# A cross-attention and routed-experts kernel on Trainium2: how rows enter a batch of attention, where gates are ordered, and in what order results are gathered

## The chip, the cores and the metric

The kernel runs on 1 core of one Trainium2 chip. The metric is the device time of that core in microseconds (us), lower is better. Below, PE is TensorE (PEld its weight loads), DVE is VectorE, ACT is ScalarE, POOL is GpSimd, SP is SyncE; a row that ends its engine's name in q is one of the engine's sequencer, mostly a DMA that it issues.

## The reference, cut to what matters

Eight batches of 512 latents (256 wide) attend to 1024 context rows each with 16 heads of 64; the result goes through a router that picks 8 of 64 experts for each of the 4096 tokens.

```python
def attention(latents, context):              # b=8, n=512, s=1024, 16 heads of 64
    lat, ctx = layer_norm(latents), layer_norm(context)
    q, k, v = lat @ Wq, split(ctx @ Wkv)
    k = apply_rope(k, cos, sin)
    attn = softmax(clip(q k^T / 8, -11, 11))
    return (attn v) @ Wo + bo

x = x + tanh(g_xattn) * attention(layernorm(x), ctx)
xf = layernorm(x)
scores = sigmoid(xf @ router_w.T)             # 4 of 8 groups, then 8 of 64 experts
routed = sum over the 8 chosen e of weight_e * (relu(xf @ up[e])**2 @ down[e])
shared = relu(xf @ shared_up)**2 @ shared_down
x = x + tanh(g_ffn) * (routed + shared)
```

## The kernel before

Four stages follow each other, each a block of its own with a barrier behind it.

**setup** splits the projection weights into a high and a low part, turns the rope tables, and normalises the rows of batch 0.

**attention** (line 690) goes over 8 batches of 8 pairs of heads. A pair has eight steps c = 0 to 7. In step c of pair g the PE makes the scores of pair g-1 (L908), the projections of pair g (L939 keys, L951 queries, L924 values), the product with the values (L965), and in steps 1, 4 and 6 the denominator (L973) and the output projection (L1001) of pair g-2. ACT takes the exponential (L1043) and copies projections out of PSUM, POOL clips the exponentials (L1147) and finishes keys (L1143), DVE sums exponentials (L1336), does rope (L1320, L1321), the low halves (L1326, L1308) and 1/denominator (L1311, L1313). The value projection runs in the first two of every four pairs; the last two have less work for the PE. Since a loop always has a pair before it, the first pair attends to a zeroed pair: keys, queries, values and two exponentials are filled with zeros at the start. The routing of batch b-1 (the functions of `Router`) is spread over the pairs of batch b on DVE, and its rows are scattered to DRAM by POOL.

Between two batches stands `boundary(b)`: the PE turns the normalised rows of the new batch in three units of eight 128x128 transposes into the two score buffers (L887), ACT and DVE each apply the layer norm's gain and shift to half a unit (L1020, L1278), ACT writes the high part (L1024), DVE the low part (L1285). The new batch's first scores wait for it, since the buffers are those of the scores. Batch 0 is a hardware loop of its own, that normalises one tile at a time; the later batches normalise two.

**finish_routing** does the shared expert for all tokens and routes the last batch. DVE there also orders the gates: for each of 32 tiles of tokens three operations of 128x512 (compare the slots with the keys, multiply with the gates, reduce to 8 gates). Tiles 0 to 15 are wholly DVE's (L1568, L1570, L1571); for tiles 16 to 31 (`by_pool`) the multiplication is POOL's (L1443), between DVE's L1578 and L1588, into space that is free only after the last scatter.

**experts** goes over 320 blocks of 128 rows. For each block the PE turns the rows (L1814), multiplies with the up weights (L1787) and the down weights (L1807); DVE does relu and square (L1845, L1849) and every second copy to the result ring (L1839), ACT the other copies. SP loads rows, stores results in groups of four blocks (L1716), and loads the down weights of four experts with every second one of the first 32 blocks. POOL gathers the results of a batch of tokens, 32 gathers for each of 8 batches (L1870), each of one choice k of one tile of tokens into one of 8 buffers, in the order k = 0 to 7, and DVE adds them (L1832), one gather's rows beside each block. A batch's gathers begin when all blocks that its rows may lie in have been stored:

```python
            def gather(b):
                for k in range(YR // YC):
                    pool.wait_ge(y_stored[k], (b * BODY + E_R + BODY) // YR * 16)
                for q in range(BODY):
                    t, k = q // TOP_K, q % TOP_K
```

with BODY = 32, E_R = 64, YR = 8 and YC = 4. The keys of a token are its slots sorted downwards, so k = 7 is the smallest slot, and slots of one expert's later tokens lie higher in memory.

## Time and profile before

| | us |
|---|---|
| median of 3 runs | 2625.3 (2624.1 to 2625.47) |
| the profiled execution's own time | 2619.68 |
| its span, first to last instruction | 2617.9 |
| setup, to the start of attention's block | about 33 |
| attention | to about 1992 |
| finish_routing | to about 2163 |
| experts | to 2617.9 |

The granted TensorE clock over the span is 0.957 of full speed, where 1.00 is 2.4 GHz and 0.5 is 1.2 GHz. The chain of waits and the groups of instructions give averages over stages that have different limits, so each stage is read by itself, by the timeline and by the busy time of its stretches.

### The profile page before, as it was taken

Reading aid. Unit: us, or ns where it says so; the run is one execution under the profiler, and the core shown is the slowest. Engines: PE = TensorE matmul, PEld = TensorE weight load, DVE = VectorE, ACT = ScalarE, POOL = GpSimd, SP = SyncE. Lnnn points to the kernel's source line nnn. Section 1 sums busy time; section 2 is a strip of 40 time slices with the busy share of each in tenths; the row PEclk is TensorE's granted clock in tenths of the full one; section 3 lists DMA queues with packets and bytes.
Section 4 is the critical chain, followed back from the end, with each engine's and each line's share of the span. In section 5 each row is a group of like instructions: output and inputs, shape, how many; then the busy total and the mean of one; then the engine's idle time right before and its main releaser. Section 6 shows DMA issues by size and latency. Waiting matters only on the chain. (4 is left out here: it accounts for less than half of the span.)

```text
span 2617.9 us, 41338 instructions
## 1 busy us (share of the span) xinstructions
PE 2320.2 (89%) x11459; PEld 1289.8 (49%) x11459; DVE 2104.3 (80%) x3593; ACT 1518.0 (58%) x2536; POOL 1800.0 (69%) x1569
## 2 busy tenths in 40 slices
PE   2999899999989999998999899999997958999990
PEld 1444444444544444444444444444444647988770
DVE  5687688988897897889889878988896775688884
ACT  3666666666665666666666656666662423666660
POOL 3787576679858885887698688858875630077776
PEclk9999999999999999999999999999997989999995
DMA  8434333221111111111211111111115408799994
GB/s 301 170 105 167 114 125 101 77 79 43 59 46 59 55 59 46 59 44 53 79 43 57 48 57 56 60 46 57 45 55 172 150 1 305 243 321 325 328 319 141
DMA packets 163129, 305.71 MB, mean 117 GB/s; under 512 B 19842, under 2 KB 99138, under 8 KB 160194
## 3 DMA queue, kind: packets, MB, share of 16 engines
q1 hardware_dynamic: 134786, 235.40, 26.5%
q0 software_dynamic: 24576, 67.14, 7.7%
q8 instruction: 107, 1.75, 0.3%
q14 instruction: 140, 1.15, 0.1%
q10 hardware_dynamic: 3520, 0.27, 0.1%
HBM read 172.99 MB, written 129.76 MB: 116 GB/s over the span
## 5 line engine op out<-in xcount | busy, mean ns | idle before, releaser
L1147 POOL TENSOR_SCALAR e<-e 128x1024 f32<-128x1024 f32 x520 | 682.2, 1312 | 364.5 <-ACT e L1043 311.2
L1043 ACT ACTIVATE e<-scores 128x1024 f32<-128x1024 f32 x520 | 533.2, 1025 | 443.8 <-PE scores L908 437.1
L1336 DVE TENSOR_TENSOR e_sum<-e_sum,e 128x1024 f32<-128x1024 f32 x391 | 612.7, 1567 | 107.7 <-POOL e L1147 103.1
L965 PE MATMUL ps_o<-e,v 128*64 128x512 f32 x2088 | 570.3, 625 | 6.8 <-POOL e L1147 6.8
L908 PE MATMUL scores<-q_t,k_t 64*128 64x512 f32 x3120 | 512.6, 434 | 14.4 <-ACT affine L1020 12.7
L908 PEld LDWEIGHTS scores<-q_t,k_t 64*128 64x128 f32 x3120 | 257.9, 188 | 378.5 <-issue 313.4
L1870 POOL DMA_INDIRECT more<-results_in_blocks,index x256 | 246.4, 962 | 210.6 <-DMA results_in_blocks<-more 129.4
L1055 ACT ACTIVATE k_sw<-ps_k 32x512 f32<-32x512 f32 x512 | 301.2, 588 | 83.5 <-PE ps_k L939 78.7
L1132 POOL DMA_INDIRECT rows_in_blocks<-room,a_r_index_now x192 | 265.5, 1383 | 49.0 <-issue 42.1
L939 PE MATMUL ps_k<-ctx_t,wqk 128*128 128x512 f32 x768 | 222.9, 427 | 12.5 <-DVE q_t L1308 12.2
L924 PE MATMUL ps_v<-wv,ctx_t 128*128 128x512 f32 x768 | 212.1, 411 | 0.0
L1143 POOL TENSOR_TENSOR k_c<-k_c,k_sw 128x512 f32<-128x512 f32 x128 | 194.8, 1521 | 19.9 <-DVE k_sw L1321 17.2
L965 PEld LDWEIGHTS ps_o<-e,v 128*64 128x64 f32 x2088 | 104.5, 136 | 201.4 <-issue 172.0
L1001 PE MATMUL ps_y<-wo,o_n 128*128 128x256 f32 x528 | 158.4, 425 | 48.0 <-POOL o_n L1151 46.7
L1807 PE MATMUL ps_out<-down_all,room 128*128 (+1 forms) x640 | 194.1, 385 | 3.3 <-DVE room L1849 2.4
L939 PEld LDWEIGHTS ps_k<-ctx_t,wqk 128*128 128x128 f32 x768 | 141.0, 197 | 87.2 <-issue 44.7
L1001 PEld LDWEIGHTS ps_y<-wo,o_n 128*128 128x128 f32 x528 | 94.1, 198 | 168.1 <-POOL o_n L1151 89.8
L1814 PE MATMUL ps_x<-ident,x_nat 128*128 128x128 f32 x640 | 125.4, 278 | 50.2 <-PEq L1351 27.6
L1326 DVE TENSOR_TENSOR k_t<-k_c,k_t 128x512 fp32r<-128x512 f32 x128 | 125.6, 981 | 53.7 <-ACT k_t L1068 53.5
L924 PEld LDWEIGHTS ps_v<-wv,ctx_t 128*128 128x128 f32 x768 | 134.2, 188 | 69.8 <-issue 47.0
L1770 ACT ACTIVATE x_nat<-ps_x 128x256 f32<-128x256 f32 x320 | 121.2, 379 | 76.9 <-PE ps_x L1814 73.4
L1832 DVE SCALAR_TENSOR_TENSOR x<-more,gate,x 128x256 f32<-128x256 f32 x256 | 123.1, 481 | 48.0 <-DMA more<-results_in_blocks,index 46.6
(294 smaller groups left out, 3612.3 us busy)
## 6 DMA issues: line engine op xcount, KB each, us to landing
rows_in_blocks<-room SPq DMA_DIRECT2D x16, 2560.0 KB, 10.1
x_nat<-rows_in_blocks SPq DMA_DIRECT2D x160, 256.0 KB, 5.2
results_in_blocks<-more SPq DMA_DIRECT2D x80, 512.0 KB
wqk<-wqk_pairs SPq DMA_DIRECT2D x65, 512.0 KB, 3.5
wv<-wv_quads SPq DMA_DIRECT2D x17, 1024.0 KB, 4.9
wo<-in_L_xattn_Wo SPq DMA_DIRECT2D x66, 128.0 KB, 3.4
x_nat<-in_ctx SPq DMA_DIRECT2D x8, 1024.0 KB, 7.7
down_all<-in_L_ffn_down_w SPq DMA_DIRECT2D x16, 512.0 KB, 8.2
```

What stands on the lines that cost most here:

```text
L908: mm = pe.matmul(scores[:, c % 2, hh * N:(hh + 1) * N], k_t[rows, att, kp, c * P:(c + 1) * P], q_t[rows, att, qp, :], start=(part == 0), s ...
L924: mm = pe.matmul(ps_v[:], ctx_t[:, a, cc, tile * P:(tile + 1) * P], wv[:, bb, cc], start=(k == 0), stop=(k == 5))
L939: mm = pe.matmul(ps_k[:], wqk[:, jj, bb, cc, 1], ctx_t[:, a, cc, half * N:(half + 1) * N], start=(k == 0), stop=(k == 5))
L965: mm = pe.matmul(ps_o[hh * DH:(hh + 1) * DH, :], v[:, tile, buf, hh * DH:(hh + 1) * DH], e[:, tile % 4, hh * N:(hh + 1) * N], start=(tile ...
L1001: mm = pe.matmul(ps_y[:, i, :], o_n[:, t * P:(t + 1) * P], wo[:, jj], start=True, stop=True)
L1043: act.activation(e[:, c % 4], scores[:, c % 2], ACT.Exp, scale=SCALE).then_inc(s_exp, 1)
L1055: st = act.activation(k_sw[to], ps_k[of], ACT.Copy)
L1132: pool.indirect_dma_start(xs_dram, bass.IndirectOffsetOnAxis(ap=router.index_now[:, t, k:k + 1], axis=0), router.rows[:, t], None).then_in ...
L1143: pool.tensor_tensor(k_c[:], k_c[:], k_sw[:], ALU.add).then_inc(s_turned, 1)
L1147: pool.tensor_scalar(e[:, c % 4], e[:, c % 4], EXP_HI, EXP_LO, ALU.min, ALU.max).then_inc(s_clip, 1)
L1336: dve.tensor_tensor(total, e[:, 0] if c == 2 else total, e[:, tile % 4], ALU.add).then_inc(s_sum, 1)
L1870: pool.indirect_dma_start(land[:, k], None, y_dram[0:(E_R + (b + 1) * BODY) * P, :], bass.IndirectOffsetOnAxis(ap=at, axis=0)).then_inc(y_ ...
```

## The change

**Six pieces instead of a boundary.** `boundary` is gone from all engines. The rows of the next batch are turned in six pieces of four transposes, each of 128x512 elements, into the buffer of the value projection (`ps_v`), five in steps 3 to 7 of the last pair of the batch and the sixth in step 0 of the first pair of the next. For each piece ACT applies gain and shift and writes the high part, DVE writes the low part. DVE no longer has a share of the gains.

**No empty pairs.** The first pair has no scores, exponentials, sums and outputs; the pair's code is left out where there is no pair g-1 or g-2, and the fills with zeros are gone. Semaphores are raised to the counts that would have been. Batch 0 is written out as the others are. The first five pieces of batch 0 stand ahead of the loop, and DVE waits for all rows of x behind them. SP's first loads no longer wait for the fills. The router's weights and biases are loaded and turned in `setup`.

**Order inside a pair.** At step 2 ACT takes the logarithm of the denominator ahead of the exponential, DVE's two operations for 1/denominator come right behind the sum of step 2 (before: step 3, behind the low half of the query), and at step 3 POOL multiplies with it ahead of its clip.

**Gates.** Tiles 16 to 31 are ordered in finish_routing, all by DVE, where tiles 0 to 15 were; tiles 0 to 15 are ordered in the first 48 blocks of experts, one of the three operations in each block. POOL has no part in it any more. Slots and gates are kept in halves, so four loads and two scalings stand where two loads and one scaling were.

**Gathers.** A tile's choices are gathered from k = 7 down, and the gathers for k = 7 to 4 of a batch's first tile need one group of four blocks less.

**First down weights.** The down weights of experts 0 to 3 are also loaded at the end of finish_routing, behind the scatters, into space of their own, and the first four blocks use these.

```diff
-                for k in range(YR // YC):
-                    pool.wait_ge(y_stored[k], (b * BODY + E_R + BODY) // YR * 16)
                 for q in range(BODY):
-                    t, k = q // TOP_K, q % TOP_K
+                    t, k = choice(q)
+                    n = blocks_of(b, k) // YC
+                    if q in (0, YC):
+                        for group in (n - 2, n - 1):
+                            pool.wait_ge(y_stored[group % (YR // YC)], (group // (YR // YC) + 1) * 16)
...
+        def choice(q):
+            return q // TOP_K, TOP_K - 1 - q % TOP_K
+        def blocks_of(b, k):
+            return -(-(E_R + (b + 1) * BODY - k) // YC) * YC
...
+        CHUNKS = 6
+        CHUNK_AT = {(7, 3): 0, (7, 4): 1, (7, 5): 2, (7, 6): 3, (7, 7): 4, (0, 0): 5}
...
+            def turn_rows(n, number):
+                pe.wait_ge(s_affine, 1 + number)
+                for t in range(NT):
+                    mm = pe.transpose(ps_v[:, t * P:(t + 1) * P],
+                                      x_nat[:, (0, 4, 8)[n // C2] + t, n % C2 * P:(n % C2 + 1) * P], pers.ident[:])
+                mm.then_inc(turned, 1)
...
+            def place_rows(n, number):
+                k = chunk_of(n, 0)[1]
+                act.wait_ge(turned, number + 1)
+                if not isinstance(number, int) or number >= 2:
+                    act.wait_ge(t_lo, number - 1)
+                act.activation(affine[:, n % 2], ps_v[:], ACT.Identity, bias=pers.shift[:, k, n % C2:n % C2 + 1],
+                               scale=pers.gain[:, k, n % C2:n % C2 + 1]).then_inc(s_affine, 1)
+                act.wait_ge(s_affine, 1 + number + 1)
+                act.activation(chunk_of(n, 0)[0], affine[:, n % 2], ACT.Copy).then_inc(t_hi, 1)
...
+            def split_rows(n, number):
+                dve.wait_ge(t_hi, number + 1)
+                dve.tensor_tensor(chunk_of(n, 1)[0], affine[:, n % 2], f32(chunk_of(n, 0)[0]), ALU.subtract
+                                  ).then_inc(t_lo, 1)
+            for n in range(CHUNKS - 1):
+                split_rows(n, n)
+            dve.wait_ge(x1_loaded, 16 * (B - 1))
...
+            sp.dma_start(router.rows, ins["down_w"][0:CHUNK].rearrange("e p n -> p e n")).then_inc(kept.first_loaded, 16)
...
+                if i < 3 * LATER:
+                    order(i)
```

How the change moves instructions is seen at three places. The first is the PE's program at the passage from the last pair of a batch (steps 6 and 7) to the next batch. Before (L887 are the boundary's transposes, L908 scores, L965 values, L793 the loop's turn):

```order
L908 MATMUL scores<-q_t,k_t 128x512 x6
L965 MATMUL ps_o<-e,v 64x512 x2
L1001 MATMUL ps_y<-wo,o_n 128x256 x2
L908 MATMUL scores<-q_t,k_t 128x512 x6
L965 MATMUL ps_o<-e,v 64x512 x2
L793 UNCONDITIONAL_BRANCH
L793 ISA
L880 ISA
L887 MATMUL scores<-ident,x_nat 128x128 x16
L883 ISA
L887 MATMUL scores<-ident,x_nat 128x128 x8
```

and after (L881 are the transposes of one piece, L903 the scores, L968 values):

```order
L903 MATMUL scores<-q_t,k_t 128x512 x6
L881 MATMUL ps_v<-ident,x_nat 128x128 x4
L968 MATMUL ps_o<-e,v 64x512 x2
L1004 MATMUL ps_y<-wo,o_n 128x256 x2
L903 MATMUL scores<-q_t,k_t 128x512 x6
L881 MATMUL ps_v<-ident,x_nat 128x128 x4
L968 MATMUL ps_o<-e,v 64x512 x2
L813 UNCONDITIONAL_BRANCH
L813 ISA
L896 REGISTER_ALU
L897 ISA
L903 MATMUL scores<-q_t,k_t 128x512 x6
```

The 24 transposes in a row have become groups of four between the scores and the product with the values of a step.

The second place is DVE's program at the end of finish_routing and the beginning of experts. Before (L1568 to L1571 order one tile, L1845 and L1849 are the first blocks' relu and square; ahead of these rows stand the 16 tiles shared with POOL):

```order
L1568 TENSOR_TENSOR cells<-more,key 128x512
L1570 TENSOR_TENSOR cells<-cells,more 128x512
L1571 TENSOR_REDUCE gate<-cells 128x8
L1351 UNCONDITIONAL_BRANCH
L1825 UNCONDITIONAL_BRANCH
L1845 TENSOR_SCALAR room<-ps_hid 128x128
L1849 TENSOR_TENSOR room<-room 128x128
L1845 TENSOR_SCALAR room<-ps_hid 128x128
L1849 TENSOR_TENSOR room<-room 128x128
```

and after (L1522 to L1525 order one tile, L1506 adds the shared expert's result, L1798 and L1801 are the first two parts of ordering a tile in the first blocks):

```order
L1525 TENSOR_REDUCE gate<-cells 128x8
L1506 SCALAR_TENSOR_TENSOR x<-ps_s,gates,x 128x512 x2
L1310 UNCONDITIONAL_BRANCH
L1776 UNCONDITIONAL_BRANCH
L1810 TENSOR_SCALAR room<-ps_hid 128x128
L1814 TENSOR_TENSOR room<-room 128x128
L1798 TENSOR_TENSOR e_cells<-more,key 128x512
L1810 TENSOR_SCALAR room<-ps_hid 128x128
L1814 TENSOR_TENSOR room<-room 128x128
L1801 TENSOR_TENSOR e_cells<-e_cells,more 128x512
```

No ordering is left behind the last addition of the stage, and one part of it stands in each of the first 48 blocks.

## Rows read from the trace of the kernel before

**Rows 1.** The page: the span and TensorE's busy time (share) and instructions.

```profile
span 2617.9 us, 41338 instructions
PE 2320.2 (89%) x11459; PEld 1289.8 (49%) x11459; DVE 2104.3 (80%) x3593; ACT 1518.0 (58%) x2536; POOL 1800.0 (69%) x1569
```

**Rows 2.** ACT's exponentials by stretch: stretch, length, busy (count), granted clock, DMA share, GB/s.

```profile
1446.80:1482.10 35.30, 8.20 (x8) 0.92 0.10 32
1928.00:1953.70 25.70, 8.21 (x8) 1.00 0.15 47
```

**Rows 3.** Stretches: length; PE, PEld, DVE, ACT, POOL busy (count); clock, DMA share, GB/s.

```profile
1242.20:1273.10 30.90, 30.48 (x135) 15.20 (x136) 25.41 (x37) 19.39 (x28) 16.25 (x12) 0.97 0.18 56
...
1927.80:1953.80 26.00, 23.48 (x112) 10.16 (x110) 25.66 (x30) 16.16 (x22) 20.15 (x15) 1.00 0.15 46
```

**Rows 4.** PE's timeline at a boundary: start, us, line, operation [idle before <-releaser].

```profile
1477.11 1.94 PE L887 MATMUL scores<-ident,x_nat 128*128 128x128 f32 x8 [3.17 <-DVE affine L1278]
1480.47 1.65 PE L908 MATMUL scores<-q_t,k_t 64*128 64x512 f32 x6 [1.42 <-ACT affine L1020]
```

**Rows 5.** Single lines: count, ns min/median/max, first and last start, shapes.

```profile
L1020 ACT ACTIVATE affine<-scores,shift,gain x24: 758/762/779, 51.5 to 1720.6; 128x512 f32<-128x512 f32 x24
L1024 ACT ACTIVATE ctx_t<-affine x32: 612/630/634, 52.4 to 1720.1; 128x512 fp32r<-128x512 f32 x32
L1285 DVE TENSOR_TENSOR ctx_t<-affine,ctx_t x32: 676/682/687, 54.8 to 1721.5; 128x512 fp32r<-128x512 f32 x32
L1326 DVE TENSOR_TENSOR k_t<-k_c,k_t x128: 674/938/1573, 73.8 to 1953.8; 128x512 fp32r<-128x512 f32 x128
```

**Rows 6.** PE's waits over the span: who for whom, us in total, times, longest.

```profile
PE ps_y L1001 <- POOL o_n L1151: 46.7, 37, 4.6
...
PE ps_k L939 <- DVE q_t L1308: 12.2, 6, 2.0
```

**Rows 7.** The timeline at the start of attention.

```profile
39.70 0.34 SPq L808 DMA_DIRECT2D wqk<-wqk_pairs  x1
...
60.08 2.39 ACT L1055 ACTIVATE k_sw<-ps_k 32x512 f32<-32x512 f32 x4 [0.46 <-PE ps_k L939]
60.19 1.74 DVE L1336 TENSOR_TENSOR e_sum<-e_sum,e 128x1024 f32<-128x1024 f32 x1 [0.75 <-DMA x<-in_x]
...
64.63 1.66 PE L951 MATMUL ps_k<-lat_t,wqk 128*128 128x512 f32 x6
...
87.91 1.03 ACT L1043 ACTIVATE e<-scores 128x1024 f32<-128x1024 f32 x1 [0.88 <-PE scores L908]
```

**Rows 8.** The timeline at the end of finish_routing.

```profile
2128.47 7.17 PE L1480 MATMUL ps_s<-sdn,h_g 128*128 128x256 f32 x32 [1.35 <-ACT h_g L1512]
...
2135.68 0.75 DVE L1552 SCALAR_TENSOR_TENSOR x<-ps_s,gates,x 128x512 f32<-128x512 f32 x1 [2.63 <-PE ps_s L1480]
...
2163.22 1.88 PE L1814 MATMUL ps_x<-ident,x_nat 128*128 128x128 f32 x6 [27.58 <-PEq L1351]
```

**Rows 9.** The comparison of one tile's slots, and its timeline neighbours in a block of experts.

```profile
L1568 DVE TENSOR_TENSOR cells<-more,key x16: 677/691/694, 2060.7 to 2160.5; 128x512 f32<-128x512 f32 x16
...
2205.27 0.29 DVE L1845 TENSOR_SCALAR room<-ps_hid 128x128 f32<-128x128 f32 x1 [0.48 <-PE ps_hid L1787]
2205.59 0.29 DVE L1849 TENSOR_TENSOR room<-room 128x128 f32<-128x128 f32 x1
2205.80 0.42 DVE L1839 COPY more<-ps_out 128x256 f32<-128x256 f32 x1
```

**Rows 10.** The blocks' copies L1770 by stretch: columns as in rows 2.

```profile
2163.90:2205.90 42.00, 12.21 (x32) 0.94 1.05 366
...
2205.90:2223.40 17.50, 6.10 (x16) 1.00 0.74 244
```

**Rows 11.** The gathers: line as in rows 5, then the first in the timeline.

```profile
L1870 POOL DMA_INDIRECT more<-results_in_blocks,index x256: 940/946/1212, 2284.8 to 2611.4; - x128
...
2284.80 1.12 POOL L1870 DMA_INDIRECT more<-results_in_blocks,index  x1 [129.44 <-DMA results_in_blocks<-more]
```

498 lines of the change are left out of this document (215 added, 283 removed).

## The prediction, made before the changed kernel ran

> **What bounds the kernel now.** I read the page first: TensorE is busy 89% of a span of 2617.9 us [rows 1]. That is an average over stages, so next come the stages one by one, in stretches and in the timeline. In attention the PE is busy 30.48 of 30.9 us in the first pair of a batch [rows 3], so a pair with value projections is the PE's. The last pair of a batch has none, and there DVE is busy 25.66 of 26.0 us and the PE 23.48 [rows 3]: that pair is DVE's. Behind it stands the boundary. The last pair with a boundary behind it takes 35.3 us, the very last pair, which has none, 25.7 us [rows 2]. In those 9.6 us the PE waits 3.17 us for DVE's share of the gains and 1.42 us for ACT's, and then makes its scores in 1.65 us [rows 4]; the granted clock over the pair and its boundary is 0.92, against 1.00 in the pair without one [rows 2]. At the start of attention the PE has nothing before the fills and router loads are done: the second pair's first exponential starts at 87.91 us [rows 7]. At the end of finish_routing the PE is done, DVE adds the last product at 2135.68 us, and the next stage's first matmul starts at 2163.22 us after 27.58 us of idle PE [rows 8]; between them DVE only orders gates. In experts the gathers are one chain on POOL: 256 of them from 2284.80 to 2611.4 us, (2611.4 - 2284.8) / 255 = 1.28 us each [rows 11], with the rest of the blocks beside them. So what comes before the first gather moves the end, and what comes after it hardly does.
>
> **Start of attention.** The first load is issued at 39.70 us, and DVE waits at 60.19 us for the last rows of x [rows 7]: 20.5 us. Changed, SP issues the first load right behind the barrier, at about 33.2 us, and is 1.7 us shorter, since the three router loads are in setup, where they lie beside larger loads. The rows land at 33.2 + 20.5 - 1.7 = 52.0 us. The first five pieces are done by then (each of them some 1.7 us, from about 34.5 us), so DVE's wait for x is what ends last. Then the first pair, which has no attention to hide behind, runs as a chain. DVE splits the sixth piece and multiplies with the cosine, 0.68 us each as the same shape takes in [rows 5]: 53.4. Query projection 1.66 [rows 7]: 55.0. ACT's copy 0.63, DVE's low half 0.68 [rows 5]: 56.3. Second half of the keys 1.66: 58.0. ACT swaps the key halves in 2.39 us [rows 7] while the first of three value tiles waits to be copied out of the one buffer: 60.4 + 0.6; the two further tiles take 1.66 + 0.63 + about 0.1 of signalling each: 65.6. Scores, about 1 us: the second pair's first exponential starts at 66.6 us instead of 87.9. That is **-21.3 us**. If x did not bind, the same chain would begin 8 us earlier (-29); if it landed as late as now, it would be -13.
>
> **Boundaries.** Seven of them go. What goes with each is 9.6 us [rows 2], and about 0.5 us of slow matmuls in the first step behind it (scores at 1.65 us [rows 4]). What comes for it are six pieces. On the PE each is four transposes; eight take 1.94 us at the slow clock [rows 4], so half a microsecond at the full one, five times 2.5 us, and the PE has 2.5 us of room in the last pair [rows 3]. ACT gets 0.76 + 0.63 = 1.39 us a piece [rows 5], five times 7 us, on 16.16 of 26.0 us [rows 3]: it fits. DVE has no room: 25.66 of 26.0. It gets five low halves. The same subtraction takes 0.682 us at the boundary, where POOL stands still, and 0.938 us as the median among pairs, up to 1.573 [rows 5]. I take 0.94, since the pieces now stand among POOL's clips: 5 x 0.94 = 4.7 us in the last pair. The sixth falls into a pair that the PE bounds [rows 3] and costs nothing as long as that is so. So each boundary becomes 4.7 us, net 10.1 - 4.7 = 5.4, seven times **-37.8 us**. The last batch had no boundary, but turns rows that nobody uses: **+4.7 us**.
> The Trainium skill, page "SBUF — State Buffer", section "Who interferes with whom", speaks against the change here: a DVE instruction with two SBUF inputs contends with a GpSimd instruction that reads SBUF, by an exclusive lock. The two rows for one shape, 0.682 and 0.938 us, agree with it. With 0.68 for each of the five halves the last pair would be 1.3 us shorter, over eight batches 10 us; by the rule the longer value holds.
>
> **Order inside a pair.** POOL's product ahead of its clip takes away some of the PE's waits for it, 46.7 us over the span in 37 places; 1/denominator ahead of the query's low half lengthens the waits for that one, 12.2 us in 6 places [rows 6], where DVE is late, by the two operations of 0.68 us each. It also lets a clip wait where the product is late. I take 0, with 15 us either way at most.
>
> **End of finish_routing.** The 16 tiles with POOL and three tiles behind them leave; the three that stay between the last two groups take 3 x 3 x 0.69 = 6.2 us [rows 9], which is less than the 7.17 us of the products alone that the PE works on meanwhile [rows 8]. The stage ends with DVE's addition at 2135.68 + 0.75 = 2136.4 instead of 2162.7: -26.3 us. The PE's wait of 1.35 us before the last products [rows 8] falls to the usual half microsecond, as DVE is not late any more: -0.8. The extra loads and the extra scaling, five short operations of about 1 us in all, lie beside the PE's matmuls; the scatters end some 50 us before the stage does. Together **-27.1 us**. The early load of four experts' down weights costs nothing there and takes a possible wait from block 0; the other loads are as they were.
>
> **First blocks of experts.** Each of 48 blocks gets one operation of 0.69 us [rows 9] on DVE. A block has relu to square 0.32 us and square to the next start 0.21 us [rows 9], and each second one the copy of 0.42. With 0.61 to 0.69 for the new part a block takes DVE 0.32 + 0.21 + 0.65 + 0.2 = 1.35 to 1.4 us. The first 32 blocks take 42.0 us now, 1.31 each, at a DMA share of 1.05: there the loads bound them [rows 10], and 32 x 1.34 is about 43. The next 16 take 17.5 us, 1.10 each [rows 10]; they become 21.2. Together **+4.7 us**, and everything up to the first gather moves with it. At the bounds: 0, if DVE's part hides behind the loads and in the PE's lag, and 48 x 0.69 = 33 us if nothing hides.
>
> **Gathers.** The first gather may start one group of four blocks earlier, 4 x 1.10 = **-4.4 us** [rows 10]; the fifth waits for the next group, which is 4.4 us later, and four gathers take 5.1 us. The chain behind it has as many gathers as before. Bounds: 0 and -5.
>
> **Sum.** -21.3 - 37.8 + 4.7 + 0 - 27.1 + 4.7 - 4.4 = -81.2 us. The profiled execution took 2619.7 us, 1.8 more than its span and 5.6 less than the median of the runs; on that median, 2625.3 - 81.2 = 2544.1 us.
>
> **Rivals.** All keep the start, the stage end and the gathers (-21.3 - 27.1 + 4.7 - 4.4 = -48.1) and differ in what six pieces cost, x, against 10.1 us a boundary: -48.1 + 7 (x - 10.1) + x.
> *Pieces hidden.* DVE's lag in the last pair is carried into the next pair, where DVE is busy only 25.41 of 30.9 us [rows 3]; then x is 2 or less. For it: nothing but the next denominator waits for DVE's sums. Against it: that denominator comes in step 1. With x = 2: 2625.3 - 102.8 = 2522.5 us.
> *Pieces as dear as the boundary.* DVE late by 1/denominator as well, the PE waiting for the query's low half, ACT held up behind a turn that waits for the piece before. x = 10.1: 2625.3 - 38.0 = 2587.3 us. For it: that pair already holds the PE's waits for the low half of the query.
> *Slower.* One buffer, one affine tile of two halves and in-order queues make each piece a serial chain on the path: transposes 0.5, gains 0.76, high part 0.63, low part 0.94, 2.83 us; six make x = 17.0. Then 2625.3 - 48.1 + 48.3 + 17.0 = 2642.5 us. It decides against the change from x = 15.6, where -48.1 + 7 x 5.5 + 15.6 is +6. Against it: the scores have buffers of their own, so PE, ACT and DVE can work on different pieces.
> *Ordering exposed.* As forecast, but the first blocks lose 15 to 33 us instead of 4.7, if the added part delays each relu, and with it the PE's next block: 2554 to 2572 us. Against it: two blocks are in flight between PE and DVE.
>
> **How the numbers follow.** Forecast 0.57 (its own range 2530 to 2558), hidden pieces 0.19, dear pieces 0.09, exposed ordering 0.12, slower 0.03. The range 2515 to 2575 takes in the hidden pieces, the start at either bound (+8, -8) and most of the exposed ordering; it leaves out the dear pieces and the slower case, about 0.15 with what lies below. About 0.2% (5 us) is what a measurement of this kernel can tell from no change. Faster by more than that 0.96, within it 0.01, slower 0.03.
>
> **What would show it.** Right: the second pair's first exponential near 66.6 us; eight exponentials of a batch's last pair in 30 to 31 us with DVE full; PE idle for about 1 us instead of 27.58 at the start of experts; 32 blocks in about 43 us and 16 in 21; gathers again at 1.28 us each. Wrong: PE waits on ACT or DVE lines of the pieces, a last pair above 33 us, a wait of DVE for x that ends past 55 us, or blocks above 1.5 us each while the gates are ordered.

## The result and the profile after

The changed kernel takes 2555.4 us (median of 4 runs, 2553.0 to 2559.0); the kernel before took 2624.7 us beside it (4 runs, 2622.7 to 2625.5). The ratio is 0.9738, with a 95% interval of 0.9721 to 0.9755, and 69 us are gone where 81 were forecast. The profiled execution has a span of 2551.4 us for 2617.9 [rows 1]. One execution behind the medians below is left out: the fourth of number_late took 2639.5 us at a granted clock of 0.835, where its other three had 0.97.

The page, its span and first lines (columns as in rows 1):

```profile
span 2551.4 us, 40379 instructions
PE 2294.6 (90%) x11366; PEld 1273.0 (50%) x11366; DVE 2055.1 (81%) x3571; ACT 1524.2 (60%) x2556; POOL 1734.6 (68%) x1515
```

TensorE has 25.6 us less to do and still shows 90%: the average says next to nothing here, as before. So the two traces are laid side by side by stage. Each number of this table is the difference, after minus before, between two events of the profiled executions:

| stretch | forecast us | measured us |
|---|---|---|
| up to the second pair's first exponential (87.91, 67.02) | -21.3 | -20.9 |
| from there to the last pair of batch 0 (162.7, 156.0 long) | 0 | -6.7 |
| from there to the attention tail's first exponential (1953.8, 1906.0) | -33.1 | -20.2 |
| from there to the first block of experts (2163.9, 2091.8) | -27.1 | -24.3 |
| from there to the first gather (120.9, 120.7 long) | +4.7 - 4.4 | -0.2 |
| first to last gather (326.6, 332.3 long) | 0 | +5.7 |
| sum | -81.2 | -66.6 |

The third row and the last one are off by 12.9 and 5.7 us, and the second one, which was to be 0, takes 6.7 us back. For the third row, the exponentials of a last pair and of the pair 0 behind it (columns as in rows 2):

```profile
923.70:956.90 33.20, 8.18 (x8) 0.95 0.10 34
956.90:988.30 31.40, 8.26 (x8) 1.00 0.17 56
1875.10:1906.00 30.90, 8.19 (x9) 0.94 0.12 40
```

The very last pair, which had taken 25.7 us [rows 2], takes 30.9; the one with a pair 0 behind it 33.2, where the forecast was 30.4. It is the dearest of its kind; the seven take 31.3 us in the mean. The same stretches with all engines (columns as in rows 3):

```profile
923.70:956.90 33.20, 29.73 (x142) 14.16 (x144) 31.41 (x35) 22.49 (x32) 19.30 (x16) 0.95 0.10 34
1875.10:1906.00 30.90, 28.12 (x134) 12.87 (x134) 29.21 (x32) 22.41 (x33) 19.28 (x16) 0.94 0.12 40
```

DVE is busy 31.41 of 33.2 us, so the pair is still DVE's; but the PE has become dearer too, 28.1 us for 23.48 [rows 3], at a granted clock of 0.94 for 1.00. Four transposes at 0.66 us, five times, are 3.3 of these 4.6 us (the forecast had 0.5 us for each four). Another 0.9 stands behind one wait, where four matmuls of the product with the values take 1.98 us for 1.08. PE's waits over the span, as in rows 6:

```profile
PE ps_k L944 <- DVE q_t L1264: 34.1, 20, 2.7
...
PE ps_y L1004 <- POOL o_n L1135: 17.8, 9, 3.6
```

The wait for POOL's product went from 46.7 to 17.8 us, the wait for the query's low half from 12.2 to 34.1. That fits the new order inside the pair, which the forecast had put at 0; the experiments test it. One such wait, first on the PE, then in DVE's queue (timeline, columns as in rows 4):

```profile
939.47 2.50 PE L944 MATMUL ps_k<-ctx_t,wqk 128*128 128x512 f32 x6 [2.71 <-DVE q_t L1264]
```

```profile
929.30 1.05 DVE L461 TENSOR_TENSOR a_r_at_next<-room,a_r_ranks 128x64 f32<-128x64 f32 x1
930.38 0.23 DVE L463 TENSOR_TENSOR a_r_over<-a_r_at_next,room 128x64 f32<-128x64 f32 x1
930.64 0.19 DVE L468 TENSOR_SCALAR a_r_opened<-a_r_over 128x64 f32<-128x64 f32 x1
930.87 3.44 DVE L471 SCALAR_TENSOR_TENSOR a_r_opened<-a_r_over,a_r_opened 128x64 f32<-128x64 f32 x3
934.26 1.23 DVE L1286 TENSOR_TENSOR e_sum<-e 128x1024 f32<-128x1024 f32 x1
935.40 0.68 DVE L1289 TENSOR_TENSOR o_n<-ps_y,r_den 128x512 f32<-128x512 f32 x1
936.12 0.69 DVE L1291 SCALAR_TENSOR_TENSOR r_den<-o_n,r_den 128x512 f32<-128x512 f32 x1
936.73 2.09 DVE L478 TENSOR_TENSOR a_r_opened<-a_r_opened 128x64 f32<-128x64 f32 x3
938.74 0.68 DVE L1264 TENSOR_TENSOR q_t<-ps_k,q_t 128x512 fp32r<-128x512 f32 x1
```

DVE has no gap in these rows. In the last pair the router's block counts (L461 to L478) stand in step 1 and 2, and the low half of the query, whose high half ACT had finished at 932.4 us, comes at 938.74 behind all of it. The PE stands still for 2.71 us, and the projection behind the wait takes 2.50 us, at a granted clock of 0.62, where it takes 1.65 at the full clock.

### The profile page after: what moved, and what is told of

It is laid out like the page before. It is cut to its first block and busy times, and to the rows that moved or that the text cites. A ratio compares the mean times of both kernels' runs of the same rounds, so it can differ in the third digit from the quotient of the medians.

```text
span 2551.4 us, 40379 instructions
## 1 busy us (share of the span) xinstructions
PE 2294.6 (90%) x11366; PEld 1273.0 (50%) x11366; DVE 2055.1 (81%) x3571; ACT 1524.2 (60%) x2556; POOL 1734.6 (68%) x1515
## 3 DMA queue, kind: packets, MB, share of 16 engines
q1 hardware_dynamic: 135234, 235.93, 27.1%
## 5 line engine op out<-in xcount | busy, mean ns | idle before, releaser
L1139 POOL TENSOR_SCALAR e<-e 128x1024 f32<-128x1024 f32 x512 | 689.8, 1347 | 357.5 <-ACT e L1047 303.6
L1047 ACT ACTIVATE e<-scores 128x1024 f32<-128x1024 f32 x512 | 525.1, 1026 | 410.9 <-PE scores L903 398.2
L1286 DVE TENSOR_TENSOR e_sum<-e_sum,e 128x1024 f32<-128x1024 f32 x384 | 585.7, 1525 | 160.7 <-POOL e L1139 151.9
L968 PE MATMUL ps_o<-e,v 128*64 128x512 f32 x2048 | 560.8, 626 | 7.0 <-POOL e L1139 6.6
L903 PE MATMUL scores<-q_t,k_t 64*128 64x512 f32 x3072 | 499.9, 431 | 4.7 <-issue 4.7
L903 PEld LDWEIGHTS scores<-q_t,k_t 64*128 64x128 f32 x3072 | 251.4, 186 | 365.2 <-issue 293.2
L944 PE MATMUL ps_k<-ctx_t,wqk 128*128 128x512 f32 x768 | 219.4, 422 | 34.1 <-DVE q_t L1264 34.1
L968 PEld LDWEIGHTS ps_o<-e,v 128*64 128x64 f32 x2048 | 102.7, 136 | 192.1 <-issue 161.1
L1004 PE MATMUL ps_y<-wo,o_n 128*128 128x256 f32 x512 | 154.6, 427 | 21.1 <-POOL o_n L1135 17.8
L1004 PEld LDWEIGHTS ps_y<-wo,o_n 128*128 128x128 f32 x512 | 92.1, 200 | 138.4 <-issue 94.8
L1734 PE MATMUL ps_hid<-x_nat,room 128*128 128x128 f32 x1024 | 156.5, 275 | 2.0 <-DVE room L1810 1.2
```

The lines of the kernel that those rows point to most:

```text
L903: mm = pe.matmul(scores[:, c % 2, hh * N:(hh + 1) * N], k_t[rows, att, kp, c * P:(c + 1) * P], q_t[rows, att, qp, :], start=(part == 0), s ...
L944: mm = pe.matmul(ps_k[:], wqk[:, jj, bb, cc, 1], ctx_t[:, a, cc, half * N:(half + 1) * N], start=(k == 0), stop=(k == 5))
L968: mm = pe.matmul(ps_o[hh * DH:(hh + 1) * DH, :], v[:, tile, buf, hh * DH:(hh + 1) * DH], e[:, tile % 4, hh * N:(hh + 1) * N], start=(tile ...
L1004: mm = pe.matmul(ps_y[:, i, :], o_n[:, t * P:(t + 1) * P], wo[:, jj], start=True, stop=True)
L1047: act.activation(e[:, c % 4], scores[:, c % 2], ACT.Exp, scale=SCALE).then_inc(s_exp, 1)
L1139: pool.tensor_scalar(e[:, c % 4], e[:, c % 4], EXP_HI, EXP_LO, ALU.min, ALU.max).then_inc(s_clip, 1)
```

## The experiments

All times are medians; the kernel before, run beside them, had medians of 2622.4 to 2623.5 us. Where an effect has a place of its own, it is read there. For the batches this table gives, per kernel, the seven last pairs that have a batch behind them, the seven pairs 0 behind those, and the very last pair, all from first exponential to first exponential in the profiled execution, and their sum:

| kernel | median us | ratio, 95% interval | seven last pairs | seven pairs 0 | very last pair | sum |
|---|---|---|---|---|---|---|
| before | 2624.7 | | 248.1 | 216.2 | 25.8 | 490.1 |
| changed | 2555.4 | 0.9738 (0.9721 to 0.9755) | 219.0 | 224.2 | 30.9 | 474.1 |
| no_pieces | 2529.9 | 0.9646 (0.9627 to 0.9665) | 204.3 | 213.4 | 29.6 | 447.2 |
| no_low | 2546.8 | 0.9711 (0.9691 to 0.9730) | 218.5 | 219.1 | 30.6 | 468.2 |
| pieces_early | 2554.8 | 0.9736 (0.9719 to 0.9752) | 224.1 | 221.4 | 31.8 | 477.3 |
| den_back | 2521.8 | 0.9620 (0.9604 to 0.9636) | 202.0 | 215.6 | 27.8 | 445.3 |
| order_back | 2539.8 | 0.9678 (0.9662 to 0.9694) | 206.5 | 218.1 | 28.6 | 453.1 |
| before_order | 2642.9 | 1.0072 (1.0052 to 1.0092) | 265.3 | 219.9 | 28.7 | 513.8 |
| number_late | 2536.5 | 0.9676 (0.9657 to 0.9696) | 205.4 | 221.7 | 28.3 | 455.4 |
| low_on_pool | 2540.1 | 0.9689 (0.9673 to 0.9705) | 215.9 | 218.4 | 29.4 | 463.8 |
| start_and_last | 2509.8 | 0.9569 (0.9553 to 0.9585) | 200.4 | 217.4 | 24.0 | 441.8 |
| finish_late | 2505.7 | 0.9551 (0.9538 to 0.9564) | 196.7 | 214.4 | 23.0 | 434.1 |
| gates_back | 2583.7 | 0.9851 (0.9831 to 0.9871) | 217.2 | 225.3 | 30.6 | 473.0 |
| gather_old | 2553.6 | 0.9735 (0.9719 to 0.9752) | 218.9 | 224.9 | 30.6 | 474.4 |

The last two have the attention of the changed kernel, unchanged, so their sums show what one profiled execution differs from another by: 473.0 to 474.4. Not every profile lies near its median: den_back's took 2515.3 us, 6.5 less than the median of its four.

**Are the pieces too dear, or is it the order?** First the pieces were taken away as a whole, then DVE's part of them.

```diff
-                    turn_rows(n, number)
+                    if left_out(b, p):
+                        pe.wait_ge(s_affine, 1 + number)
+                        pe.sem_inc(turned, 1)
+                    else:
+                        turn_rows(n, number)
...
-                    place_rows(*chunk)
+                    # the same on ACT: wait for turned, count s_affine and t_hi
...
-                    split_rows(*chunk)
+                    # the same on DVE: wait for t_hi, count t_lo (in no_low this one alone)
```

> The six pieces of every batch are left out (their transposes, gains, high and low halves; only the counting of their semaphores stays), but for the first six at the start; so every batch attends to the rows of the first, and the routing that comes of it is another one. To be read is the first exponential of the attention tail, 1906.0 us in the changed kernel. The prediction had 33.1 us less for boundaries and pieces, and the traces show 20.3 less. Theory one, the pieces are dearer than the 4.7 us a batch that were forecast: with 7 (x - 10.1) + x = -20.3 they cost x = 6.3 us a batch, and without them the tail's first exponential comes 8 x 6.3 = 50 us earlier, near 1856. Rival, the pieces cost the forecast 4.7 us and the missing 12.8 us are the new order inside the pair (1/denominator ahead of the query's low half): then 8 x 4.7 = 38 us earlier, near 1868.

Measured: the tail's first exponential at 1882.2 us, 23.8 earlier, which is 3.0 us a batch. Both theories fall: with the new order the pieces cost less than even the forecast's 4.7 us a batch, and without any the very last pair still takes 29.6 us, where the kernel before takes 25.8. PE's wait for the query's low half is all there without pieces:

```profile
PE ps_k L952 <- DVE q_t L1277: 37.3, 20, 3.9
```

> Only the low halves of the pieces on DVE are left out in the loop (six a batch; the transposes, the gains and the high halves stay), so the low halves of the rows stay those of the first batch. Read at the tail's first exponential, 1906.0 us. Theory one, the last pair is DVE's and a piece costs what DVE does for it: 5 x 0.94 us in each last pair and what the sixth costs in the next, 40 to 50 us in all, so 1856 to 1866. Rival, a piece is a serial chain through ACT and the one buffer (gains 0.76, high half 0.63), and DVE's part is hidden: less than 15 us, so 1891 or later.

Measured: 1902.4 us, 3.6 earlier. That is the rival's number, though perhaps not for its reason: with the changed order PE waits for the query's low half in any case, and the same edit with the old order, which would tell, was not run.

**Other places for the pieces.**

```diff
-        CHUNK_AT = {(7, 3): 0, (7, 4): 1, (7, 5): 2, (7, 6): 3, (7, 7): 4, (0, 0): 5}
+        CHUNK_AT = {(7, c): c - 1 for c in range(1, CHUNKS + 1)}
...
```

> All six pieces stand in the batch's last pair, in steps 1 to 6 instead of 3 to 7 and the next batch's step 0 (the order of them becomes first half of the context, queries' rows, second half). Theory one: pair 0 after a boundary (31.3 to 33.7 us against 30.9 to 31.3 before) pays for the sixth piece and for what the last pair hands over, and the last pair, DVE's, pays 0.94 us for each piece: pair 0 falls by about 1.5 us, the last pair rises by 0.9; over seven batches -4 us, at the very last batch +0.9: the whole 2 to 5 us faster. Rival: the pieces in steps 1 and 2 stand in front of the query projection, 1/denominator and its two waits, and the last pair lengthens by more than the 1.5 us: 0 to 10 us slower.

Measured: 2554.8 us, no difference. Over seven batches pair 0 gets 2.8 us shorter and the last pair 5.1 us longer, partly made up elsewhere. Of these two placements, with the new order, neither is better.

**The order inside the pair.** On DVE alone it goes back:

```diff
@@ DVE, step 2, behind the sum
-                if c == 2 and tail:
-                    dve.wait_ge(s_seed, g + 1)
-                    dve.tensor_tensor(o_n[:], y_flat, r_den[:], ALU.mult).then_inc(s_part, 1)
-                    ...
@@ DVE, step 3, behind the query's low half
+                if c == 3 and tail:
+                    dve.wait_ge(s_seed, g + 1)
+                    ...
```

> On DVE alone the two operations of 1/denominator go back behind the low half of the query, one step later; on ACT and POOL the order stays the changed one. Theory one, that move costs: the PE's key projection waited 34.1 us in 20 places for that low half (12.2 us in 6 before); with the move undone this falls to about 12, the whole is 10 to 20 us faster. Rival, it moves the wait: POOL's product, now ahead of its clip, gets 1/denominator later and holds up the clip, and the PE's value products with it; PE waits for clips and for POOL's product rise by as much or more: 0 to 20 us slower.

Measured: 2521.8 us, 33.6 faster, more than theory one gave it. The same place of the same batch, DVE and PE:

```profile
920.35 3.43 DVE L471 SCALAR_TENSOR_TENSOR a_r_opened<-a_r_over,a_r_opened 128x64 f32<-128x64 f32 x3
923.72 1.22 DVE L1292 TENSOR_TENSOR e_sum<-e 128x1024 f32<-128x1024 f32 x1
924.87 0.74 DVE L478 TENSOR_TENSOR a_r_opened<-a_r_opened 128x64 f32<-128x64 f32 x3
925.52 0.68 DVE L1264 TENSOR_TENSOR q_t<-ps_k,q_t 128x512 fp32r<-128x512 f32 x1
926.12 0.68 DVE L1267 TENSOR_TENSOR o_n<-ps_y,r_den 128x512 f32<-128x512 f32 x1
```

```profile
926.26 1.67 PE L944 MATMUL ps_k<-ctx_t,wqk 128*128 128x512 f32 x6
```

From the sum to the query's low half DVE now takes 1.80 us instead of 4.48. Two operations of 0.68 us explain 1.4 of the 2.7. The other 1.35 is the numbering of blocks (L478), 0.74 us for 2.09: with 1/denominator late, POOL stands still beside it (it ends a clip at 923.45 us and starts its product at 927.62), and the three operations run undisturbed. The PE does not wait, and its projection takes 1.67 us. POOL's wait for 1/denominator is the longer for it, but PE's waits for POOL's product are 20.9 us in all, 17.8 in the changed kernel. The last pair of batch 0, beside which DVE has nothing to route yet, takes 27.2 us in both kernels; that of the fourth batch, shown above, takes 33.2 and 29.7. So in the last pairs the move costs only in the batches that route, with the router's operations in DVE's queue as well. The cost is not confined to the last pairs: of the 28.8 us between the two sums in the table, 17.0 are in the seven last pairs, 8.6 in the pairs 0 and 3.1 in the very last one. POOL's wait in den_back:

```profile
927.62 1.64 POOL L1135 TENSOR_TENSOR o_n<-o_raw,r_den 128x256 f32<-128x256 f32 x1 [4.17 <-DVE r_den L1269]
```

With the order back on all three engines:

```diff
@@ besides den_back: ACT, step 2
                     act.activation(q_t[:, jj, 0], ps_k[:], ACT.Copy).then_inc(s_qe, 1)
+                # the logarithm and the exponential of 1/denominator, from ahead of it
@@ POOL, step 3
+                # the product o_n behind the clip, from ahead of it
```

> The whole order inside the pair is the old one again: on DVE 1/denominator behind the query's low half, on ACT its logarithm and exponential behind the query's copy, on POOL the product behind the clip. The run with DVE's part alone undone (called den_back) took 2521.8 us, 33.6 less than the changed kernel. Theory one, DVE's part is the whole cost, and what ACT and POOL got is a small gain of its own (the PE's waits for POOL's product were 46.7 us before and 17 with the product ahead of the clip): this run is 5 to 25 us slower than den_back, 2527 to 2547. Rival, the order hurts on each engine, ACT and POOL too: this run is faster than den_back, below 2520 us.

Measured: 2539.8 us, 18.0 slower than den_back. Theory one holds: beside DVE's old order, what ACT and POOL got is a gain of 18.0 us; on top of that, what DVE got is a loss of 33.6, and the whole order costs 15.6 us. (DVE's move alone, without ACT's and POOL's, was not run in the changed kernel, so the two parts are told in this order only.) PE's wait for the product is back:

```profile
PE ps_y L1004 <- POOL o_n L1139: 48.3, 40, 4.6
```

And the new order in the kernel before, without pieces, start or gates:

```diff
@@ the kernel before: ACT, step 2, ahead of the step's exponential; its second half behind it
+                    act.activation(r_den[:], y_flat, ACT.Ln).then_inc(s_log, 1)
@@ DVE, from step 3 to step 2, behind the sum; POOL, step 3, ahead of the clip
+                    dve.tensor_tensor(o_n[:], y_flat, r_den[:], ALU.mult).then_inc(s_part, 1)
+                    pool.tensor_tensor(o_n[:, 0:D], o_raw[:, 0:D], r_den[:, 0:D], ALU.mult).then_inc(s_on, 1)
```

> The kernel before with one edit, the new order inside the pair on ACT, DVE and POOL. Theory one: DVE's move costs in the last pair, where the router's block counts stand in DVE's queue as well, whether there are pieces or not (the changed kernel without pieces takes 10.3 us in step 4 of that pair, with DVE's move undone it is 5.2 us): the kernel before becomes 20 to 35 us slower, about 2650, and its last pairs 3 to 4 us longer. Rival: the cost comes only of pieces and order together, both on DVE in one pair: the kernel before stays within 8 us of 2624.

Measured: 2642.9 us, 18 to 20 slower, just short of theory one's 20 to 35 and far from the rival's 8, and close to the 15.6 that it costs in the changed kernel. Its last pairs are 2.5 us longer each, less than theory one had (3 to 4), pair 0 another 0.5. The waits trade in the same way (12.2 and 46.7 before, [rows 6]):

```profile
PE ps_k L939 <- DVE q_t L1308: 34.2, 19, 3.9
...
PE ps_y L1001 <- POOL o_n L1147: 17.1, 8, 3.6
```

Does it take 1/denominator to make the low half late, or only a long queue?

```diff
-                if (p, c) == (7, 2):
+                if (p, c) == (7, 3):
                     router.number_blocks(dve, range(0, 3))
```

> One edit to the changed kernel: the router's numbering of blocks, three operations on DVE, moves from step 2 to step 3 of the last pair, so that it stands behind the query's low half; 1/denominator stays ahead of it. Theory one: the PE waits for that low half because of all that is queued ahead of it on DVE, whichever it is; 2.1 us less of it (three operations of 0.7 us with POOL busy) take 2 us off the wait in each of seven last pairs and about 0.9 us off the projection behind it, which ran at the low clock (2.50 us for 1.66): 14 to 20 us faster, step 4 of the last pair 8.6 to about 6 us. Rival: it is the chain of 1/denominator itself (the seed from ACT, then two operations, POOL behind them) that sets step 4, and the numbering only fills a wait: less than 4 us.

Measured: 2536.5 us, 18.9 faster, and step 4 of the last pair 5.4 us for 8.5 in the mean of the six batches that route. Theory one holds: moving other work from ahead of the low half helps too, so it does not take 1/denominator.

**The start of experts.**

```diff
+            for k in range(GT):
+                dve.wait_ge(router.scattered[k], 16 * TOP_K * N_G)
+            order(range(0, LATER))
@@ experts
-                if i < 3 * LATER:
-                    order(i)
```

> The sixteen tiles of gates that the changed kernel orders in the first 48 blocks of experts are ordered at the end of finish_routing instead, by DVE alone (the kernel before had POOL's help there and took 27.6 us of idle PE); all else as changed. Theory one, as predicted: 48 operations of 0.69 us stand on the path at the stage's end, 33 us more between DVE's last addition and the first block, and the first 64 blocks get faster again, 81.4 back to 77.2 us: 33 - 4.2 = 29 us slower, near 2584. Rival: the head start of the blocks is given back later, as it was with the gathers, since the gathers' chain waits for stored groups: less than 20 us slower.

Measured: 2583.7 us, 28.3 slower. The first block's wait, 35.95 us for 1.11, and the first 64 blocks, 77.2 us for 81.5, bear out both terms. They make 30.6 us; in the trace 2.8 of them are given back behind the ninth gather (312.1 us to the last one, for 314.9), much less than the rival had:

```profile
2125.82 1.09 PE L1768 MATMUL ps_x<-ident,x_nat 128*128 128x128 f32 x4 [35.95 <-PEq L1310]
```

**The gathers.**

```diff
-            return q // TOP_K, TOP_K - 1 - q % TOP_K
+            return q // TOP_K, q % TOP_K
...
-            return -(-(E_R + (b + 1) * BODY - k) // YC) * YC
+            return E_R + (b + 1) * BODY
```

(and the waits for the stored groups once ahead of each batch, as in the kernel before.)

> In experts the gathers go again from the largest slot down, each batch of them behind all the groups of blocks that it may need; all else as changed. The first gather then starts about 4.4 us later against the first block (120.7 us after it in the changed kernel). Theory one, the head start is given back: in the changed kernel the first 32 gathers took 48.3 us for 44.0 before, waiting for stored groups, since blocks are made no sooner; the end moves by less than 2 us. Rival, as the prediction had it, the head start reaches the end: 4.4 us slower.

Measured: 2553.6 us, the same within the interval. POOL in the changed kernel, its first, its eighth and its ninth gather; then the eighth and ninth with the old order:

```profile
2212.53 1.00 POOL L1839 DMA_INDIRECT more<-results_in_blocks,index  x1 [171.89 <-DMA results_in_blocks<-more]
...
2221.60 0.95 POOL L1839 DMA_INDIRECT more<-results_in_blocks,index  x1 [0.30 <-issue]
2229.93 0.95 POOL L1839 DMA_INDIRECT more<-results_in_blocks,index  x1 [7.38 <-DVE x L1783]
```

```profile
2224.88 0.95 POOL L1837 DMA_INDIRECT more<-results_in_blocks,index  x1 [0.30 <-issue]
2228.95 0.94 POOL L1837 DMA_INDIRECT more<-results_in_blocks,index  x1 [3.13 <-DVE x L1783]
```

The head start is given back, but not where theory one had it. The ninth gather needs the place of the first one in SBUF, so it waits for DVE's first addition, and that stands in DVE's program behind block 112 (64 + 32 + 16), wherever the gathers are. Counted from the first block, the first gather starts after 120.7 us (125.3 with the old order), the ninth after 138.2 (138.4).

**The start of attention and the last batch.**

```diff
@@ DVE
-            dve.wait_ge(x1_loaded, 16 * (B - 1))
...
+                    if isinstance(b, int) and b == 0 and p == 1 and c == 0:
+                        dve.wait_ge(x1_loaded, 16 * (B - 1))
@@ the loop
-            with eng.Fori(2, B) as b:
-                batch(b)
+            with eng.Fori(2, B - 1) as b:
+                batch(b)
+            with eng.Fori(B - 1, B) as b:
+                batch(b)          # without pieces, norms and the load of the next batch
```

> Three edits to the changed kernel. 1/denominator on DVE is back behind the query's low half (2521.8 us as the only edit). DVE's wait for the rows of x of the later batches moves from ahead of the loop to their first reader, the moments in pair 1 of batch 0. The last batch gets a copy of the loop of its own, without the pieces, the load and the normalising of a batch that does not come. Each can be read in its own place. The start: x lands at 51.5 us in the changed kernel while DVE is ready at about 47.2; theory one, the second pair's first exponential comes 4 us earlier, near 63; the rival, x takes the wait along to whichever reader and the PE's slow clock sets the pair: less than 1 us. The last batch's last pair takes 27.8 us in the run with the only edit; theory one, 25.7 to 26, as in the kernel before, and another 0 to 3 us from the normalising in pairs 3 and 5; rival, a third copy of the loop's code has to be fetched and eats the gain. Together 2514 by theory one, 2522 by the rivals.

Measured: 2509.8 us, 12.0 faster than den_back. At the start the rival is right, 66.6 us for 67.4. In the changed kernel x is what DVE waits for; without that wait it waits for ACT's swap, behind a projection at the lower clock, and is 0.4 us earlier:

```profile
51.53 0.69 DVE L1163 TENSOR_TENSOR ctx_t<-affine,ctx_t 128x512 fp32r<-128x512 f32 x1 [4.71 <-DMA x<-in_x]
52.14 0.68 DVE L1270 TENSOR_TENSOR k_c<-ps_k,cos_t 128x512 f32<-128x512 f32 x1
```

```profile
48.37 0.69 DVE L1168 TENSOR_TENSOR ctx_t<-affine,ctx_t 128x512 fp32r<-128x512 f32 x1 [1.29 <-ACT ctx_t L1026]
51.72 0.69 DVE L1282 TENSOR_TENSOR k_c<-ps_k,cos_t 128x512 f32<-128x512 f32 x1 [2.66 <-ACT k_sw L1070]
```

(Nine kernels with one and the same start have 67.0 to 68.0 us there, this one and finish_late 66.6 and 66.5.) The last batch gives the larger part: its last pair takes 24.0 us instead of 27.8, and its eight pairs 223.7 instead of 230.7, 7.0 us less; it leaves out three things at once, and they are not told apart. Where the other 4 us of the 12.0 lie, these profiles do not show.

**Low halves on POOL.**

(Besides DVE's edit of den_back.)

```diff
@@ POOL, last pair, behind the clip (and no longer on DVE)
+                    pool.wait_ge(t_hi, number + 1)
+                    pool.tensor_tensor(chunk_of(n, 1)[0], affine[:, n % 2], f32(chunk_of(n, 0)[0]), ALU.subtract
+                                       ).then_inc(t_lo, 1)
```

> Two edits to the changed kernel: 1/denominator on DVE is back behind the query's low half (2521.8 us as the only edit), and the low halves of the five pieces in the last pair are made by POOL instead of DVE, behind its clip of the step. The last pair is DVE's, and the next pair's first key projection waits 1.7 us for a low half that DVE makes late, with POOL idle for 2.2 us and 3.1 us around it. Theory one: DVE has 5 x 1.2 us less, POOL 5 x 1.5 us more and room for it; each last pair and the pair behind it lose 2 to 3 us together: 15 to 25 us faster than 2521.8. Rival: POOL's subtraction stands ahead of the next clip, and the contended operations on both engines take as much longer as is saved: within 8 us of 2521.8, or slower.

Measured: 2540.1 us, 18.3 slower than den_back. The rival, and worse. Its DVE and POOL in the second half of a last pair:

```profile
947.24 2.31 DVE L1298 TENSOR_TENSOR e_sum<-e_sum,e 128x1024 f32<-128x1024 f32 x1 [1.02 <-POOL e L1139]
```

```profile
943.96 1.18 POOL L1147 TENSOR_TENSOR o_n<-o_raw,r_den 128x256 f32<-128x256 f32 x1
945.22 1.90 POOL L1139 TENSOR_SCALAR e<-e 128x1024 f32<-128x1024 f32 x1
947.20 1.27 POOL L1144 TENSOR_TENSOR ctx_t<-affine,ctx_t 128x512 fp32r<-128x512 f32 x1
948.42 2.25 POOL L1131 TENSOR_TENSOR k_c<-k_c,k_sw 128x512 f32<-128x512 f32 x1
```

POOL has next to no gap in these rows, DVE waits for clips (191.0 us over the span, for 162.9 in den_back), and PE for POOL's products (33.3 us for 20.9). DVE's sum takes 2.31 us where it takes 1.22 alone. In this pair DVE's operations add up to 29.7 us, in den_back's to 31.0: of the 5.7 us that low halves took in it there, some 4.4 came back through operations that both engines run at once.

**DVE's work out of its full stretch.**

(Besides the three edits of start_and_last.)

```diff
-        FINISH = (1, 2, 4, 6, 7)
+        FINISH = (3, 4, 5, 6, 7)
...
                 if part == 0:
                     router.r, router.k = r, numbered[0]
-                    router.number_blocks(dve, range(3, 6))
+                    router.number_blocks(dve, range(0, 6))
...
                 if (p, c) == (7, 2):
-                    router.number_blocks(dve, range(0, 3))
                     numbered[0] = router.k
```

> The three edits of the run start_and_last (2509.8 us) and a fourth: the router's numbering of blocks on DVE, three operations in step 2 of the last pair and three in step 1 of the next pair 0, all moves to step 3 of pair 0, and the two parts of slot work behind it one step later each (steps 4 and 5 for 2 and 4). In start_and_last DVE has no idle time from step 6 of pair 6 to step 3 of pair 0, and the last pair takes 29.7 us where the PE has work for 26. Theory one: what counts is DVE's work in that full stretch, wherever it stands in it; 4.8 us less of it (2.1 in the last pair, 2.7 in pair 0) make the last pair and pair 0 together 2 to 4 us shorter, seven times: 2482 to 2496 us. Rival: the slot work ends later, POOL's wait for the slots at the start of pair 1 holds up its clips, and pair 1 (29.3 us) pays what the others gain: within 4 us of 2509.8.

Measured: 2505.7 us (5 runs, 2503.4 to 2509.3), 4.1 faster than start_and_last and so between the theories, nearly the rival's; the intervals of the two ratios overlap. In the batches the gain is there, 3.7 us over the last pairs and 3.0 over pairs 0, about 1 us each time and not the 2 to 4 of theory one; pair 1 stays at 29.3 to 30.0 us, so the rival's place is wrong. The attention tail, from its first to its last exponential, takes 24.6 us for 22.2; whether the later slot work is the cause is not shown, for the three kernels with one and the same attention have 23.1, 25.8 and 25.9 us there. It has the lowest median of this study, 49.7 us faster than the changed kernel and 4.5% faster than the one before.

## Why the prediction was right, and where its steps were not

The time came out 11 us above the forecast and inside its range, in part by luck. In the trace 14.6 us are missing. Three misses add to it, the third row of the table with 12.9 us, the gathers with 5.7 and finish_routing with 2.8; the 6.7 us that batch 0 lost unforeseen take half of the first away. With the order inside the pair undone, order_back takes 2539.8 us, 4 below the forecast. Of the signs of being wrong that the prediction named, one came: two of the seven last pairs are above 33 us. Step by step:

- **What bounds the kernel** held. The last pair is DVE's, and the reading that a last pair with no boundary would cost 25.7 us plus the pieces is borne out once the order is back: in order_back the last pairs, pairs 0 and the very last pair sum to 453.1 us, 37.0 less than before, where -37.8 + 4.7 = -33.1 were forecast. With 10.1 us a boundary gone, that leaves 4.2 us a batch for the pieces, where the forecast had 4.7: right, a little too careful. It was right by a sum whose parts were not: DVE's five low halves take 5.0 to 6.5 us in a last pair of the changed kernel and 7.2 in most of den_back, not 4.7, so some of it hides.
- **Start of attention** held to 0.4 us (67.02 for 66.6), partly by luck. (The forecast's own chain adds up to 66.8: 60.4 + 0.6 and two times 2.39 are 65.8.) DVE's wait for x ended at 51.53 us for the forecast 52.0. The pieces took 1.98 us each for the assumed 1.7 and the first projections 2.91 us for 1.66, at the lower clock. The forecast's bound, 8 us earlier if x did not bind, was wrong: the PE's and ACT's chain ends within half a microsecond of x, as start_and_last shows.
- **Not forecast**: batch 0 is another 6.7 us shorter up to its last pair. 5.1 of them are in the first of these pairs (24.2 us for 29.4), which has no pair g-2 to finish any more.
- **Order inside a pair** is the step that failed. It took 0 with 15 us either way; undoing it gives 15.6 us, at the edge of that. The two directions were named rightly, but their sizes were not: in den_back and order_back the gain by ACT and POOL is 18.0 us, the loss by DVE 33.6. The forecast sized the loss by the wait as it stood (12.2 us in 6 places), plus two operations of 0.68 us. It left out that these stand in the one pair that its own first part had called DVE's, behind the router's operations; that POOL's product, which then starts earlier, lengthens DVE's operations beside it (the three of the numbering from 0.74 to 2.09 us); and that the PE comes out of some of these waits at the lower clock.
- **End of finish_routing**: -24.3 for -27.1. The PE is idle 1.11 us for 27.58 [rows 8], DVE's last addition is at 2090.24 us. The 0.8 us at the last products did not come:

```profile
2083.03 7.17 PE L1434 MATMUL ps_s<-sdn,h_g 128*128 128x256 f32 x32 [1.35 <-ACT h_g L1466]
...
2091.31 0.63 PE L1765 MATMUL ps_x<-ident,x_nat 128*128 128x128 f32 x4 [1.11 <-PEq L1310]
```

  Their wait is for ACT, not for DVE, and it is 1.35 us as before. From the tail's first exponential to DVE's last addition it is 184.3 us for 181.9, and where these 2.4 us come from is open. The early load of the first down weights was not tried by itself.
- **First blocks**: +4.2 us over 96 blocks for +4.7 (116.6 for 112.4). The parts were less right than the sum. Rows 10 after:

```profile
2092.50:2135.90 43.40, 11.84 (x31) 0.92 1.03 357
2135.90:2155.20 19.30, 6.10 (x16) 1.00 0.65 207
2155.20:2173.90 18.70, 6.10 (x16) 1.00 0.73 240
```

  The second stretch has 19.3 us for the forecast 21.2, and the third 18.7 for 17.6 before, 1.1 us that no term had. The added part takes 0.68 us, as in rows 9:

```profile
2104.00 0.68 DVE L1798 TENSOR_TENSOR e_cells<-more,key 128x512 f32<-128x512 f32 x1
```

- **Gathers**: the first one is 4.4 us earlier against the blocks, as forecast, and that is worth nothing. The forecast followed the waits for stored groups up to the fifth gather and not the wait for a free place at the ninth. From the ninth to the last gather it is 314.9 us for 313.6; those 1.3 us are within what two executions differ by (gather_old: 313.0).
- **The rivals**: "slower" needed x = 15.6 us a batch for the pieces; they cost 3.0 with the new order and some 4.2 with the old. The reason against it, buffers of their own for the scores, is consistent with that. The same numbers rule out "dear pieces" (10.1) and speak against "pieces hidden" (2 or less). "Ordering exposed" is ruled out by the 4.2 us of the first blocks.

## What to carry to other kernels

On an engine that is full over a stretch even a mere exchange of two operations can cost more than their duration: here two of 0.68 us put ahead of a third made it 2.7 us later where the router's work stood in the queue, and cost nothing in the last pair of batch 0, where it did not. Before calling a reordering neutral, look up what else the queue holds in the fullest pair, not in the mean one. Moving work to the engine next door was no relief here, since the two slow each other down. A head start counts only up to the next wait that is tied to something else: follow the chain past as many steps as there are buffers.

## What the runs showed of the hardware

DVE operations with both inputs in SBUF are much longer while POOL works on SBUF. The numbering of blocks, 64 elements wide, has the same 42 operations in both kernels; first the changed one, then den_back (count, ns min/median/max):

```profile
L478 DVE TENSOR_TENSOR a_r_opened<-a_r_opened x42: 211/722/1342, 461.8 to 1911.8; 128x64 f32<-128x64 f32 x42
```

```profile
L478 DVE TENSOR_TENSOR a_r_opened<-a_r_opened x42: 210/226/1350, 458.8 to 1879.4; 128x64 f32<-128x64 f32 x42
```

With no POOL instruction beside it none of them takes more than 227 ns, in 8 cases of the changed kernel and 26 of den_back. The longest in the changed kernel are six times as long: six of them, 1317 to 1342 ns, all beside POOL's addition of the key halves.

The low halves of the pieces show it for 512 elements. These are the five of the last pair from 923.7 us on, two for the queries' rows and three for the context's:

```profile
L1163 DVE TENSOR_TENSOR ctx_t<-affine,ctx_t x3: 678/686/1753, 949.0 to 956.5; 128x512 fp32r<-128x512 f32 x3
L1163 DVE TENSOR_TENSOR lat_t<-affine,lat_t x2: 679/946/1214, 940.9 to 943.7; 128x512 fp32r<-128x512 f32 x2
```

Together they are 5.0 us; over the eight last pairs the five take 5.65 us in the mean, 1.13 each, so the forecast's 0.94 was too little. A DVE operation with one input in PSUM shows nothing of the kind. The query's low half is of the same shape, and 28 of its 64 stand beside a clip, a product or an addition of POOL's:

```profile
L1264 DVE TENSOR_TENSOR q_t<-ps_k,q_t x64: 676/682/692, 56.5 to 1890.1; 128x512 fp32r<-128x512 f32 x64
```

What counts is what POOL does at that moment (beside nothing but its scatters, twelve low halves of keys took 673 to 692 ns), and the order inside a pair decides that: the same three operations take 2.09 us in one order and 0.74 in the other. The Trainium skill, page "SBUF — State Buffer", section "Who interferes with whom", says that a DVE instruction with both inputs in SBUF contends with a GpSimd instruction that reads SBUF; the traces agree, and the forecast, which had cited it for the pieces, did not apply it to the order.

A wait of the PE can be paid for a second time, by the granted clock behind it. The full level is 2.4 GHz and the lower one 1.2. Behind the 2.71 us wait at 939.47 us, with the PE all but without a gap for 12 us before it, the granted clock was 0.62: the projection took 2.50 us for 1.65, and the four matmuls behind it 1.82 for 1.08. It does not follow each time. Of the twelve waits of 1.8 to 2.7 us for the query's low half in the changed kernel, five were followed by both at the full level, 2.7 us together, and seven by 3.7 to 4.3 us. Without pieces six of the waits are 3.9 us, and each was followed by a slow projection, 2.65 to 2.93 us.
